# A transformer layer on one core: five f32 products of 128 stationary columns written as four products of 32 columns

## Time and profile before

| | us |
|---|---|
| median of 3 runs | 1040.51 |
| lowest, highest | 1036.64, 1040.9 |
| the profiled execution's own time | 1042.75 |
| its span | 1041.0 |
| granted TensorE clock over the span | 0.978 |

### The profile page before, as it was taken

How to read it: one execution, slowest core, us unless ns; L and a number is a source line. 1 busy time by engine, 2 the same in 40 slices (tenths; PEclk the granted TensorE clock), 3 DMA queues, 4 the chain that set the end, 5 groups by cost and what they waited for, 6 DMA issues and landing times.

```text
span 1041.0 us, 37708 instructions
## 1 busy us (share of the span) xinstructions
PE 945.6 (91%) x16095; PEld 538.6 (52%) x16095; DVE 847.4 (81%) x2112; ACT 764.4 (73%) x1042; POOL 282.7 (27%) x264
## 2 busy tenths in 40 slices
PE   3688899999999999999999999999989999999796
PEld 1334555555555555555545555555545545555454
DVE  3978978989798898989898988989898987864633
ACT  2166577777877788788878778788877777787681
POOL 6101222223132231323232321323232232223212
PEclk8689989999999999999999999999999999999999
DMA  5344334356436171735436261725445161505130
GB/s 141 77 117 106 94 104 93 89 139 168 101 97 171 48 191 44 199 60 164 105 104 165 72 166 42 207 53 162 106 131 138 51 177 43 125 3 133 63 73 21
DMA packets 94345, 112.98 MB, mean 109 GB/s; under 512 B 15201, under 2 KB 81889, under 8 KB 94177
## 3 DMA queue, kind: packets, MB, share of 16 engines
q1 hardware_dynamic: 94176, 110.56, 40.7%
HBM read 55.22 MB, written 54.53 MB: 105 GB/s over the span
## 4 chain that ended last, share of the span: by engine, by line
PE 56%; DVE 21%; ACT 13%; issue 5%; DMA 2%; SPq 1%; POOL 1%; POOLq 0%; DVEq 0%; ACTq 0%
PE acc L749 19%; DVE rowmax L1108 10%; PE pool L732 9%; ACT prob L957 7%; PE pool L609 5%; PE pool L660 4%; PE pool L624 3%; PE pool L785 3%; PE pool L676 3%; PE pool L809 2%; PE pool L794 2%; ACT vals_a L943 2%; PE pool L700 2%; ACT vals_b L943 1%; DVE xn L1066 1%
## 5 line engine op out<-in xcount | busy, mean ns | idle before, releaser
L957 ACT ACTIVATE prob<-pool 128x1024 f32<-128x1024 f32 x576 | 566.5, 1030 | 114.0 <-PE pool L676 110.0
L1108 DVE TENSOR_REDUCE rowmax<-pool 128x2 f32<-128x1024 f32 (+7 forms) x480 | 357.0, 790 | 45.5 <-PE pool L676 42.8
L749 PE MATMUL acc<-prob,vals_a 128*32 128x64 f32 (+7 forms) x2048 | 167.5, 418 | 0.0
L749 PE MATMUL acc<-prob,vals_b 128*32 128x512 f32 (+7 forms) x2048 | 161.7, 414 | 3.4 <-issue 1.9
L660 PE MATMUL pool<-stack_ka,stack_qa 48*64 48x512 bf16 (+7 forms) x2048 | 117.2, 297 | 36.9 <-DVE rowmax L1108 10.9
L676 PE MATMUL pool<-mask_t,ident_b 64*64 64x128 bf16 (+1 forms) x2304 | 128.5, 213 | 0.0
L732 PE MATMUL pool<-stack_qa,stack_ka 51*64 51x512 bf16 (+7 forms) x2048 | 108.6, 294 | 14.5 <-DVE rowmax L1108 7.6
L732 PE MATMUL pool<-stack_qb,stack_kb 48*64 48x512 bf16 (+7 forms) x2048 | 108.8, 292 | 7.0 <-DVE rowmax L1108 4.1
L1319 POOL TENSOR_TENSOR rstd<-mv,minus_half 128x4 f32<-128x4 f32 x64 | 65.6, 1024 | 154.0 <-DVE mv L1061 154.0
L660 PEld LDWEIGHTS pool<-stack_ka,stack_qa 48*64 48x64 bf16 x2048 | 43.5, 107 | 96.9 <-issue 49.6
L1331 POOL TENSOR_TENSOR parts_q<-rest_q,parts_q 128x512 bf16<-128x512 f32 x32 | 37.1, 1160 | 187.6 <-DVE parts_q L1082 187.6
(11 more groups left out here) (131 smaller groups left out, 1413.9 us busy)
## 6 DMA issues: line engine op xcount, KB each, us to landing
stack_qa<-scratch_qa SPq DMA_DIRECT2D x64, 192.0 KB, 3.9
stack_ka<-scratch_ka SPq DMA_DIRECT2D x64, 192.0 KB, 4.3
stack_kb<-scratch_kb SPq DMA_DIRECT2D x64, 192.0 KB, 4.6
stack_qb<-scratch_qb SPq DMA_DIRECT2D x64, 192.0 KB, 5.4
scratch_qa<-parts_q SPq DMA_DIRECT2D x16, 384.0 KB, 5.0
scratch_ka<-parts_k SPq DMA_DIRECT2D x16, 384.0 KB, 4.3
scratch_qb<-parts_q SPq DMA_DIRECT2D x16, 384.0 KB, 2.6
scratch_kb<-parts_k SPq DMA_DIRECT2D x16, 384.0 KB, 2.8
```

The costliest lines, as they stand in the source:

```text
L749: last = eng.matmul(acc[32 * j:32 * j + 32, BLK * blk:T], vals[a][:, blk, GROUP * g + j, :], prob[n % NPROB][:, k, at:at + T - BLK * blk], ...
L957: eng.activation(prob[n % NPROB][:, :, :], place["unit", n][0][:, :, :], ACT.Exp, scale=scale).then_inc(S["exped"], 1)
L1108: last = eng.tensor_reduce(to, of, axis=AX.X, op=ALU.max)
```

## The change

Each matmul of the five places becomes a call of `product`: four matmuls with 32 stationary columns, to PSUM partitions 0 to 31, 32 to 63, 64 to 95 and 96 to 127. What moves is the same for the four. Only the last one raises the semaphore. No step, wait, buffer, bank or slot is changed; a run of four products has 16 matmuls in the program and not 4, 32 weight loads and 32 matmuls in the trace and not 8 and 8. Over the kernel 512 products become 2,048.

```diff
--- before.py
+++ after.py
@@ -697,8 +697,7 @@
                 q.wait_ge(S["xnT" + n], b + 1)
                 for k in range(NT):
 
-                    last = eng.matmul(ps[:, P * k:P * k + P], xnT_of(n, b)[:, 1 + P * k:1 + P * (k + 1)],
-                                      heads, start=True, stop=True)
+                    last = self.product(ps[:, P * k:P * k + P], xnT_of(n, b)[:, 1 + P * k:1 + P * (k + 1)], heads)
                     if k == NT // 2 - 1:
                         yield
                 last.then_inc(S["v_" + a], 1)
@@ -782,8 +781,7 @@
                 self.warm(ps, "r" + n, b)
                 q.wait_ge(S["xr" + n], b + 1)
                 for k in range(NT):
-                    last = eng.matmul(ps[:, P * k:P * k + P], ffn["xr"][:, P * k:P * k + P], T_r[:, :],
-                                      start=True, stop=True)
+                    last = self.product(ps[:, P * k:P * k + P], ffn["xr"][:, P * k:P * k + P], T_r[:, :])
                 last.then_inc(S["r_made" + n], 1)
                 yield
                 ps, freed = place["v" + n, b]
@@ -791,8 +789,7 @@
                 self.warm(ps, "v" + n, b)
                 q.wait_ge(S["act" + n], b + 1)
                 for k in range(NT):
-                    last = eng.matmul(ps[:, P * k:P * k + P], ffn["act"][:, P * k:P * k + P], T_v[:, :],
-                                      start=True, stop=True)
+                    last = self.product(ps[:, P * k:P * k + P], ffn["act"][:, P * k:P * k + P], T_v[:, :])
                 last.then_inc(S["v_made" + n], 1)
                 yield
 
@@ -806,8 +803,8 @@
                     q.wait_ge(S["xnT3"], b + 1)
                     for k in range(2):
                         tile = 2 * half + k
-                        last = eng.matmul(ps[:, 2 * C * k:2 * C * (k + 1)], xnT_of("3", b)[:, 1 + P * tile:1 + P * (tile + 1)],
-                                          w_qk[:, :, :].rearrange("p a c -> p (a c)"), start=True, stop=True)
+                        last = self.product(ps[:, 2 * C * k:2 * C * (k + 1)], xnT_of("3", b)[:, 1 + P * tile:1 + P * (tile + 1)],
+                                            w_qk[:, :, :].rearrange("p a c -> p (a c)"))
                     last.then_inc(S["qk_made"], 1)
                     yield
 
@@ -837,7 +834,7 @@
                 self.warm(ps, "wo", b)
                 q.wait_ge(S["yT"], b + 1)
                 for k in range(NT):
-                    last = eng.matmul(ps[:, P * k:P * k + P], yT[:, P * k:P * k + P], w_ob[:, :], start=True, stop=True)
+                    last = self.product(ps[:, P * k:P * k + P], yT[:, P * k:P * k + P], w_ob[:, :])
                 last.then_inc(S["wo_made"], 1)
                 yield
```

## The result

The changed kernel takes 1033.09 us in the median of 18 runs (1028.71 to 1038.37), the one before 1037.69 in 18 (1034.8 to 1042.44). The ratio is 0.9945 with an interval of [0.9933, 0.9956], so 4.6 to 7.0 us faster, 5.7 at the ratio. The forecast was 8.5 us and 1032 us; the way was right and the gain is two thirds of the forecast. That the time is met within 1 us is luck in part: the kernel before has a median of 1037.69 us over these 18 runs and not the 1040.51 of the first three, and this error of 2.8 us and the forecast of too large a gain cancel each other. The profiled execution took 1038.37 us, its span is 1036.5; like the profiled one of before it is some 5 us above the median of its kernel.

A forecast was written before the change was run, and what follows sets the result against it. TensorE was the strongest thread, busy 91% with 56% of the chain. Its 17 us saving, x 0.67 and three quarters, gave 8.5 us: 1042.75 to 1034.2, less 2.2 for the median, 1032 us; range 1023 to 1044.

The forecast's parts named there:

- Rounds: Four narrow matmuls side by side replace each wide one; pitch about 0.11 us, streaming nearly the same, 2 us less.
- Loads and switches: Around TensorE's changed runs, fewer array-shape switches (0.095 us each) and smaller uncovered first weight loads: 15.2 us less.
- the table: Switch and load costs for the runs' 143 pieces by their neighbours; with the rounds, 17 us less of TensorE.
- a piece between a mask and 128 columns: Changed runs ahead of line 763 or 604: 0.195 us more behind them, 0.078 less for the mask in front.
- 17 us less of TensorE, half of it as time: TensorE's total saving from rounds, loads and switches was 17 us, of which 8.5 us would shorten the kernel.
- the three quarters in the forecast: Share of 11.4 us on the chain kept as time, the rest lost to VectorE and ScalarE waits: 8.5 us.
- rival 1: The saving is absorbed by waits on ScalarE and VectorE: gain 0 to 5 us, 1036 to 1041; chance 0.22.
- 0.67: Share of the changed TensorE runs taken to lie on the chain, two thirds: 17 us becomes 11.4.
- Nothing else moves: no wait, bank or transfer is added.: Outside the changed runs nothing was to change, and readers of the results find them 0.08 us earlier or more.
- Rival 2: TensorE can't be fed its 32 loads and matmuls per run fast enough; at 40 ns a pair 1060 us; chance 0.07.
- Rivals 3 and 4: Clock falls, 1040 to 1048 us, chance 0.08; the four products don't run side by side, past 1200 us, chance 0.03.

The follow-up runs named there:

- e1: The changed kernel again with no edit, against the kernel before: ratio 0.9943, 1033.77 against 1039.54 us.
- e5: The kernel before, with transfers into the score rows bringing 128 of 512 columns, the rest zero: 1045.4 us, 1.0062 of the kernel before.
- e6: The whole change, with transfers into the score rows bringing only 128 of 512 columns: 1036.37 us, 0.9977 of the kernel before.
- e4: The kernel before, with line 609's products of 512 moving columns cut into pieces of 64: 1.0234 of the kernel before, 24 us slower.
- e8: The kernel before, with line 609's products of 512 moving columns cut into pieces of 128: 1.0135 of the kernel before, 14 us slower.
- e12: e4's pieces of 64 columns on top of e5's smaller transfers: 1.0125 of the kernel before, 1.0063 against e5.
- e2: The kernel before, with only the receptance and attention b's q and k projection as four products: 0.9989 of the kernel before.
- e3: The kernel before, with only the values and output product of attention b as four products: 1.0013 of the kernel before.
- e7: The kernel before, with all places but values and output product as four products: 0.9988 of the kernel before.
- e9: The changed kernel, with the last two of a restack step's four transfers waiting for the first two: 1.0742 of the kernel before.

## Why the prediction was right, and where its size came from

- **Rounds.** Right: 0.110 us apart, eight of them 0.88 us; receptance and value product back to back at 27 ns a pair.
- **Loads and switches.** Right where the trace can show it: 59 switches fewer, as listed, and 0.07 us less for a run of `values` between masks and scores. From the last matmul ahead of each piece to the first behind it, before against after, the medians by kind of neighbours times their numbers add up to 16.8 us less, and 16.9 in e1, where the table has 17. One kind is off: a piece between a mask and 128 columns costs 0.03 us more and not 0.12.
- **17 us less of TensorE, half of it as time.** Right with thin bursts: 9.0 us measured between e5 and e6, 8.5 forecast. The interval of the 9.0 is 7 to 10 us, and the three quarters in the forecast was a choice between 0 and 1, so that it is met this closely is luck. TensorE lost ten points of the chain, VectorE gained six, waits for exponentials and maxima rose by 2.5 and 3.1 us: rival 1 is at work as a part, as the factors 0.67 and three quarters had it.
- **"Nothing else moves: no wait, bank or transfer is added."** This is the step that failed. 24 packets of instructions are added, 127 to 151, and with 256 records standing for 6.4 and not 7.65 us of work each has less time to arrive. I put the difference between 9.0 and 5.7 us, some 3 us, down to that. e5 and e6 show that the loss comes with the full bursts, and e4, e8 and e12 that records with next to no work cost time, most of it beside full bursts. Not shown is that stops make up these 3 us: the two profiles of the changed kernel have 7.6 and 1.9 us of them, the one of before 3.2.
- **Rival 2** had the right object, the feeding of TensorE, and the wrong mechanism. I looked for a tempo in the densest microsecond of the earlier trace rows and found none, rightly. The limit is in the 16 KB behind it: in the worst case the packet starts 5.3 us after TensorE has entered the block before and takes 1 us more, against a block of 6.4.
- **Rivals 3 and 4** did not come: the granted clock is 0.975 against 0.978, and four products run side by side (a round every 0.110 us).
- Open: why the parts don't add up (e2, e3, e7), and why e4 and e8 cost more than their stops. Their spans less stops are 1041.0 and 1041.1 us against 1037.8 of before. Both medians lie 2 to 3 us above their profiled executions, while that of before lies 5 us below its own; whether the other runs had more stops no trace shows.

## What to carry to other kernels

Written in the shape of the array that its neighbours use, a product costs neither a switch (0.095 us here) nor a full first weight load (0.024 us and not 0.102), so the shape of the neighbours decides. But count the instructions too: where blocks of 256 of one engine pass in 6 us beside dense transfers, as here, the packets that bring more instructions for the same work have a deadline. Look for stops with no releaser at equal distances in an engine's instruction count.

## What was not expected of the hardware

- TensorE's instructions arrive in packets of 16 KB for 256 records, one block ahead. A packet takes 0.9 to 1.9 us (one in e1 2.3), a late block is in use 1.2 to 1.6 us after landing, and beside dense transfers (some 220 GB/s) its start is put off by up to 5.3 us.
- 7,168 extra loads and matmuls that add 2.4 us of work cost 24 us (e4), or 6.5 us with a quarter of the data in the transfers into the score rows (e12).
- One wait on SyncE in the middle of each step of four transfers cost 75 us of 1,039 (e9).
